# Target rows of an attention stage kept on chip and picked by TensorE's registers, in place of rows loaded for each tile of edges

## The chip, the cores and the metric

The kernel runs on one core of one Trainium2 chip. The metric is the device time of one execution in microseconds (us); the time before is the median of three runs. A core has TensorE (PE, matrix products out of on-chip memory into the accumulation banks called `psum`), VectorE (DVE), ScalarE (ACT), GpSimd (POOL) and SyncE (SP), which issues DMAs. Each engine works through its own list of instructions in order and waits on semaphores for the others.

## The reference, cut to what matters

A graph of 3125 nodes and 50000 edges, the edges sorted by target, goes through two attention layers. The change is in the second one:

```python
x = rms_norm(x) @ W_down                       # 1024 -> 256 features
xl = (x @ Wl).reshape(n, 4, 64)                # row of a node as source
xr = (x @ Wr).reshape(n, 4, 64)                # row of a node as target
msg = xl[src] + xr[dst]                        # one row for each edge
act = where(msg > 0, msg, 0.2 * msg)
e = einsum('ehd,hd->eh', act, att)             # logits, 4 heads
alpha = softmax of e over the edges (and self loop) of one target
out = segment_sum(alpha[..., None] * xl[src], dst)
x = layernorm(x + out.reshape(n, 256) @ W_up)
```

## The kernel before, in words

The edges stand in 440 tiles of 128, four tiles make a group (`U = 4`, 110 groups), five groups a block (`BG = 5`, 22 blocks). A tile of edges has its targets within one window of 64 nodes (`WN = 64`); `wtab` holds the window number of each tile, which depends on the data. From a tile to the next it stays or goes up by one.

**Node stage** (lines 1332 to 1652). For 25 tiles of 128 nodes it finishes layer 0 and makes the rows `xl` and `xr` (256 features and 8 partial logits, `XRW = 264` words). `xl` goes to the table `xl_table` in DRAM. `xr` is written to the on-chip array `acc` (`xr[:, t, :]`) and stored from there to `xr_table` by SP (`store_xr`, L1426 to 1429). At the start of the stage SP also has the table of local target numbers copied from DRAM to DRAM in another order (L1430 to 1432).

**Fused stage** (L1672 to 2176), all engines in one loop over the groups:

- POOL gathers the `xl` rows of a group's edges, four indirect DMAs a group, into a ring of 15 groups (`RG = 15`, helper line L161). It may gather group g once group g - 15 has been weighed.
- SP loads, for every tile of edges, the 64 `xr` rows of its window into `near` (L1770, 66 KB, its address from a register), and for every block the local target numbers `lt` of 640 edges for each half of the partitions (L1762, two DMAs) and the segment masks (L1776, four DMAs).
- ACT makes the transposed one-hot matrices `onehot_t` of group g + 2 from `lt` (L1817, L1819). The two first tiles of a group stand on partitions 0 to 63, the other two on 64 to 127, so they are 128x256 for a group.
- PE (`logits`, L1874 to 1890) forms `xr[dst] + xl[src]` in `psum` by halves of a group: for two tiles `onehot_t` (64 rows) times `near` (L1884), then the identity times the ring (L1889, 128 rows).
- DVE multiplies each half by the attention vector (`product`, L2026), reduces (L2032), and adds to the logits in `finish` (L2039); ACT copies the linear part of the logits (`self_logits`, L1826) after each product and so frees the banks.
- Once for a block a segmented scan over edges gives the softmax weights `pw` (PE L1909 to 1933, DVE L2050 to 2093, ACT L1854 to 1866).
- Ten groups behind (`BACK = 10`) the rows are weighed: per group sixteen pieces of 64 columns (4 tiles, 4 heads); ACT does twelve (L1842), DVE four in one instruction (L2135). PE sums them by target with `onehot` (L1949, 16 matmuls of two 64-column halves) and DVE adds the result to `acc1` (L2112, four times a group). DVE picks the window there by a register that moves on by one bit a tile (`go_on`, L1983 to 1986); the bits are made once by `pack_moves` in block 1 (L1972 to 1981).

**Last stage**: `W_up` and the layer norm, L2227 on.

What sets the order is the text of each engine's loop (`unit`), unrolled by three blocks, and the semaphores: `s_ot` one-hot made, `s_xr` near rows landed, `s_r` gather landed, `s_pg` half a group in `psum`, `s_pd` product read, `s_sc` linear part read, `s_wa` and `s_wd` weighed by ACT and DVE.

Of the kernel before, what the change touches and what calls it, by code (L numbers as in the profile page):

```python
# [308 lines left out]
def gnn_kernel(nc, x, src, dst, w0, att_s, att_d, bias, rms_w, w_down, wl, wr, att1, w_up, out):  # L309
# [9 lines left out]
    xr_t = nc.dram_tensor("xr_table", (NP, XRW), F32, kind="Internal").ap()  # L319
    wloc2_t = nc.dram_tensor("window_local_blocks", (T // 20, 2, 10 * P), BF16, kind="Internal").ap()  # L320
# [18 lines left out]
    with top:  # L339
# [989 lines left out]
        accf = acc[:].rearrange("p t n -> p (t n)")  # L1329
        xr = accf[:, 0:NT * XRW].rearrange("p (t n) -> p t n", n=XRW)  # L1330
        att_relu = w9[:].rearrange("p t n -> p (t n)")[:, 3 * D + HID:3 * D + 2 * HID]
        with ExitStack() as ph:
# [39 lines left out]
            s_xrs = sem("n_xrs")  # L1372
            s_wl2 = sem("n_local_blocks")
# [8 lines left out]
            with nc.Block() as block:  # L1382
# [18 lines left out]
                def _(sp):  # L1401
# [31 lines left out]
                    pipelined(sp, NT, [(0, load_sums), (0, load), (0, load_down), (8, store_xr)],  # L1433
                              AHEAD, 6)
                    sp.wait_ge(s_wl2, 32)
                    sp.wait_ge(s_xrs, 16 * NT)
# [121 lines left out]
                def _(dve):  # L1558
                    sums = Chain(dve, s_zc)
                    nc.vector.tensor_scalar(isrc[:], isrc[:], int(MISS) - 1, None, ALU.bitwise_and)  # L1560
                    dve.wait_ge(S["zt"], 1)
# [93 lines left out]
        BG = 5  # L1655
        BS = BG * U
        NBLK = NG // BG
# [5 lines left out]
        acc1 = accf[:, NWP * P:NWP * P + NWP * 2 * HS].rearrange("p (w h n) -> p w h n", w=NWP, h=2)  # L1663
        FREE = NWP * (P + 2 * HS)
# [4 lines left out]
        assert FREE2 <= NT * D - 2 * D  # L1669
        s_last = [sem("f_" + n) for n in ("wu", "xl")]  # L1670
        s_x1 = [sem(f"f_x1{i}") for i in range(2)]
        with ExitStack() as ph:  # L1672
# [14 lines left out]
            in_xl = Words(accf, 0, NWP * P)  # L1687
# [3 lines left out]
            near = in_xl.take(BG * 2 * XRW).rearrange("p (s q n) -> p s q n", s=BG, q=2)  # L1691
# [52 lines left out]
            with nc.Block() as block:  # L1744
# [11 lines left out]
                def _(sp):  # L1756
# [22 lines left out]
                    def unit(u, r, k, m):  # L1779
# [5 lines left out]
                        for i in range(BG):  # L1785
# [7 lines left out]
                            if k < NBLK - 1 and i == 1:  # L1793
                                load_local(u + 1, (r + 1) % RU)
                            if i == 2:
                                load_masks(u, r)
# [582 lines left out]
```

## Time and profile before

| | us |
|---|---|
| median of three runs | 2523.01 |
| lowest, highest | 2516.96, 2532.45 |
| the profiled execution's own time | 2534.76 |
| its span, first to last instruction | 2533.1 |

| engine | busy us | share of the span |
|---|---|---|
| PE | 1896.9 | 75% |
| DVE | 1597.8 | 63% |
| ACT | 1183.2 | 47% |
| POOL | 1063.6 | 42% |

The profile comes from one execution, which took 2534.76 us; 1.66 us of it lie outside the span. Its mean granted TensorE clock is 0.891 of full speed. By the line numbers in the timeline the stages are: preparation and logits of layer 0 up to about 526 us, the first aggregation up to 1247, the node stage to 1464, the fused stage to 2425, the last stage to the end. The shares of busy time are means over these stages, so a stage has to be read by its own rows.

### The profile page before, as it was taken

The numbers are of one execution on the slowest core, as the hardware profiler recorded it, in microseconds if no ns is written. First come the engines' busy times: TensorE is split into PE (matmuls) and PEld (weight loads), VectorE is DVE, ScalarE is ACT, GpSimd is POOL, SyncE is SP. The second block draws the span as 40 slices with busy tenths as digits, with TensorE's granted clock in tenths as the row PEclk, the third lists the DMA queues.
The fourth block names the chain that finished last, engine by engine and source line by source line (L and its number), as shares of the span: only waits on it lengthen the run. The fifth ranks groups of instructions, "written<-read, shape, count | busy, mean of one in ns | idle before, by whom it ended". The sixth has DMA issues, their size and how long they took to land. (4 is left out here: it accounts for less than half of the span.)

```text
span 2533.1 us, 50983 instructions
## 1 busy us (share of the span) xinstructions
PE 1896.9 (75%) x12291; PEld 1206.5 (48%) x12291; DVE 1597.8 (63%) x4381; ACT 1183.2 (47%) x4251; POOL 1063.6 (42%) x1564
## 2 busy tenths in 40 slices
PE   5899999866777766677588924776777677777778
PEld 4455555334555444445377712444444444444443
DVE  6677777555555555555589815666666665666768
ACT  3100000246665665666566601554555554555766
POOL 1122222146666666666311162455454555454140
PEclk9999999979999999999889966888777887888779
DMA  8444433068888888888799743444344443444547
GB/s 316 107 101 111 109 103 97 33 211 286 289 287 285 292 287 290 288 286 289 232 314 330 233 127 87 109 111 110 105 112 106 115 115 106 109 109 104 97 146 264
DMA packets 209857, 456.49 MB, mean 180 GB/s; under 512 B 41915, under 2 KB 111288, under 8 KB 209648
## 3 DMA queue, kind: packets, MB, share of 16 engines
q0 software_dynamic: 90000, 281.90, 34.8%
q1 hardware_dynamic: 89008, 144.64, 19.1%
q10 hardware_dynamic: 30672, 27.93, 5.1%
q8 instruction: 70, 1.15, 0.2%
q14 instruction: 107, 0.88, 0.1%
HBM read 419.97 MB, written 47.44 MB: 185 GB/s over the span
## 5 line engine op out<-in xcount | busy, mean ns | idle before, releaser
L161 POOL DMA_INDIRECT ring<-xl_table,isrc x440 | 447.2, 1016 | 449.8 <-DVE w L2135 198.4
L1270 ACT ACTIVATE wone<-onehot,w 128x64 f32<-128x64 f32 x1760 | 433.8, 334 | 288.5 <-DVE onehot L1316 166.9
L1287 PE MATMUL banks<-w_sb,wone 128*64 128x256 f32 x2368 | 342.8, 415 | 142.9 <-DVE acc L1312 55.1
L161 POOL DMA_INDIRECT w_sb<-xp_table,isrc x296 | 297.6, 1005 | 180.0 <-PE banks L1290 107.1
L995 PE MATMUL banks<-w_sb,acc 128*128 128x512 f32 x736 | 342.1, 604 | 0.0
L1842 ACT ACTIVATE w<-ring,pw 128x64 f32<-128x64 f32 x1320 | 325.5, 335 | 0.0
L1884 PE MATMUL banks<-acc 64*128 64x264 f32 x880 | 194.4, 523 | 156.8 <-ACT lg L1826 50.8
L1312 DVE TENSOR_TENSOR acc<-banks,acc 128x512 f32 x440 | 304.5, 692 | 0.0
L1889 PE MATMUL banks<-ring,ident 128*128 128x260 f32 x880 | 301.4, 472 | 2.2 <-issue 2.2
L2026 DVE SCALAR_TENSOR_TENSOR acc<-banks,w 128x512 f32<-128x512 f32 x220 | 146.2, 686 | 238.4 <-remote 134.8
L1311 DVE TENSOR_TENSOR zacc<-banks,zacc 64x9 f32 x440 | 69.5, 158 | 330.6 <-PE banks L1290 210.5
L1287 PEld LDWEIGHTS banks<-w_sb,wone 128*64 128x64 f32 x2368 | 179.1, 145 | 198.9 <-issue 80.8
L1949 PE MATMUL banks<-w,acc 128*64 128x132 f32 x1760 | 157.9, 333 | 123.0 <-DVE w L2135 111.0
L1826 ACT ACTIVATE lg<-banks 128x16 f32<-128x16 f32 x220 | 42.7, 198 | 442.2 <-DVE acc L2026 345.0
L1889 PEld LDWEIGHTS banks<-ring,ident 128*128 128x128 f32 x880 | 175.8, 222 | 121.4 <-issue 101.5
L1287 PE MATMUL banks<-rows_c,wone 128*64 128x256 f32 x1152 | 159.9, 403 | 71.5 <-DVE acc L1312 24.7
L2112 DVE TENSOR_TENSOR acc<-banks,acc 128x132 f32 x440 | 127.3, 289 | 108.7 <-remote 72.0
L1884 PEld LDWEIGHTS banks<-acc 64*128 64x128 f32 x880 | 82.3, 224 | 232.4 <-issue 203.2
L1949 PEld LDWEIGHTS banks<-w,acc 128*64 128x64 f32 x1760 | 126.0, 166 | 138.9 <-DVE acc L2119 114.7
L995 PEld LDWEIGHTS banks<-w_sb,acc 128*128 128x128 f32 x736 | 131.2, 191 | 122.1 <-issue 122.0
L161 POOL DMA_INDIRECT rows_c<-xp_table,isrc x144 | 144.5, 1004 | 86.8 <-PE banks L1290 49.6
L931 ACT ACTIVATE zacc<-pidx 128x450 f32<-128x450 f32 x1 | 0.6, 578 | 361.9 <-DVE onehot_t L1081 361.9
(343 smaller groups left out, 2938.7 us busy)
## 6 DMA issues: line engine op xcount, KB each, us to landing
acc<-xr_table SPq DMA_DIRECT2D x440, 66.0 KB
lt_bc<-local_dst ACTq DMA_DIRECT2D x110, 128.0 KB, 3.7
w<-acc SPq DMA_DIRECT2D x100, 128.0 KB, 4.5
x_table<-y POOLq DMA_DIRECT2D x25, 512.0 KB, 7.2
acc<-x_table SPq DMA_DIRECT2D x25, 512.0 KB, 3.7
low_bc<-src_low ACTq DMA_DIRECT2D x98, 128.0 KB, 4.3
acc<-in_x SPq DMA_DIRECT2D x12, 1024.0 KB, 13.2
xp_table<-xp_st SPq DMA_DIRECT2D x24, 512.0 KB
```

The costliest lines, as they stand in the source:

```text
L161: return self.pool.indirect_dma_start(out, None, table, bass.IndirectOffsetOnAxis(ap=idx, axis=0), bounds_check=self.bound, oob_is_err=False)
L995: last = nc.tensor.matmul(psum[:, 2 * r + i], xT_all[:, u, k, :], w_sb[:, k, i * 512:(i + 1) * 512], start=(k == 0), stop=(k == KD - 1))
L1270: last = nc.scalar.activation(wone[:, s, j, h, :], onehot[:, s, j, :], ACT.Copy, scale=w9[:, bass.ds(g * U + j, 1), h:h + 1].rearrange("p ...
L1287: nc.tensor.matmul(psum[WN * a:WN * (a + 1), j, k * C:(k + 1) * C], wone[:, s, j, h, :], slots[r][:, j, h * C:(h + 1) * C], start=True, st ...
L1311: nc.vector.tensor_tensor(zv, psum[0:WN, 4 + j, 0:W9], zv, ALU.add)
L1312: nc.vector.tensor_tensor(av, psum[:, j, :], av, ALU.add).then_inc(s_acc, 1)
L1842: last = nc.scalar.activation(msg[:, s, j, h, 0:HD], ring[:, rg * U + j, h * HD:(h + 1) * HD], ACT.Copy, scale=pw[:, r2, i2 * U + j, h:h + 1])
L1884: nc.tensor.matmul(psum[:, 2 * e + j // 2, 0:XRW], onehot_t[half, rg % 3, j % 2, :], near[half, i, j % 2, :], start=True, stop=False)
L1889: last = nc.tensor.matmul(psum[:, 2 * e + j // 2, 0:XLW], ident[:], ring[:, rg * U + j, :], start=False, stop=True)
L1949: last = nc.tensor.matmul(sums_of(j)[WN * a:WN * (a + 1)], onehot[:, s, j, :], msg[:, s, j, 2 * a:2 * a + 2, :].rearrange("p h n -> p (h n)"),
L2026: nc.vector.scalar_tensor_tensor(out=prod[:, 2 * e:2 * e + 2], in0=psum[:, 2 * e:2 * e + 2, 0:HID], scalar=0.0, in1=bc(att_relu[:].unsquee ...
L2112: nc.vector.tensor_tensor(v, sums_of(j), v, ALU.add).then_inc(s_acc, 1)
```

## The change

`xr` isn't stored any more: it stays in `acc`, and the second layer's logits read it there. `onehot_t` gets one column block for each tile of edges and all 128 partitions (128x512 for a group), and its product with `xr` is a matmul of 128 rows against the tile of 128 nodes that holds the window. PE picks that tile with registers: `place` counts windows, `place >> 1` is the tile, and one bit per tile of edges moves it on. `pack_moves` is made in the node stage, so that PE and DVE both read the packed words. `lt` is one broadcast of 2560 numbers to 128 partitions for a block (640 KB) from a table that exists already. Halves of a group are now tiles 0, 1 and 2, 3. ACT weighs ten of a group's sixteen pieces, DVE six, in two instructions.

```diff
-    xr_t = nc.dram_tensor("xr_table", (NP, XRW), F32, kind="Internal").ap()
-    wloc2_t = nc.dram_tensor("window_local_blocks", (T // 20, 2, 10 * P), BF16, kind="Internal").ap()
...
-                    def store_xr(t, s, m):
-                        sp.wait_ge(S["sf"], t + 1)
-                        sp.dma_start(xr_t[bass.ds(t * P, P), :], xr[:, bass.ds(t, 1), :].rearrange("p a n -> p (a n)"))\
-                          .then_inc(s_xrs, 16)
-                    for a in range(2):
-                        sp.dma_start(wloc2_t[:, a].rearrange("b (i n) -> b i n", n=2 * P),
-                                     wloc_t.rearrange("(b i a q) e -> a b i (q e)", i=5, a=2, q=2)[a]).then_inc(s_wl2, 16)
...
-                    sp.wait_ge(s_wl2, 32)
-                    sp.wait_ge(s_xrs, 16 * NT)
...
                     nc.vector.tensor_scalar(isrc[:], isrc[:], int(MISS) - 1, None, ALU.bitwise_and)
+                    link = Chain(dve, s_pack)
...
+                    for s in reversed(range(BS - 1)):
+                        link(nc.vector.scalar_tensor_tensor(out=packed, in0=packed, scalar=2.0, in1=by_block[:, :, s],
+                                                            op0=ALU.mult, op1=ALU.add))
+                    link(nc.vector.tensor_copy(packed_i, packed))
                     dve.wait_ge(S["zt"], 1)
...
-        acc1 = accf[:, NWP * P:NWP * P + NWP * 2 * HS].rearrange("p (w h n) -> p w h n", w=NWP, h=2)
-        FREE = NWP * (P + 2 * HS)
+        acc1 = accf[:, NT * XRW:NT * XRW + NWP * 2 * HS].rearrange("p (w h n) -> p w h n", w=NWP, h=2)
+        FREE = NT * XRW + NWP * 2 * HS
...
-            onehot_t = in_wu.take(3 * 2 * P).rearrange("p (s q e) -> p s q e", s=3, q=2)
+            onehot_t = between.take(3 * U * P).rearrange("p (s j e) -> p s j e", s=3, j=U)
...
-            ACT_MORE = U
+            ACT_MORE = 2
...
                     def load_local(b, r):
                         wait(sp, s_ot, (b - RU + 1) * BG)
-                        for a in range(2):
-                            sp.dma_start(lt[WN * a:WN * (a + 1), r].rearrange("p i n -> p (i n)"),
-                                         wloc2_t[bass.ds(b, 1), a].rearrange("b n -> (b n)").partition_broadcast(WN))\
-                              .then_inc(s_lt[r], 16)
-
-                    def load_near(g, i, at):
-                        wait(sp, s_pg, 2 * (g - BG + 1))
-                        for j in range(U):
-                            half = slice(WN * (j // 2), WN * (j // 2 + 1))
-                            sp.dma_start(near[half, i, j % 2, :], xr_w[bass.ds(at[j], 1)].rearrange("w n c -> (w n) c"))\
-                              .then_inc(s_xr[i], 16)
+                        sp.dma_start(lt[:, r].rearrange("p i n -> p (i n)"),
+                                     local_t[b * BS:(b + 1) * BS, :].rearrange("s e -> (s e)").partition_broadcast(P))\
+                          .then_inc(s_lt[r], 16)
...
+                    pe.reg_mov(place, 0)
+                    pe.reg_load(words, packed_i)
+
+                    def tile_of_step(word):
+                        pe.reg_alu(moved, place, 1, ALU.logical_shift_right)
+                        tile = pe.snap(moved, min_val=0, max_val=NT - 1)
+                        pe.reg_alu(moved, word, 1, ALU.bitwise_and)
+                        pe.reg_alu(place, place, moved, ALU.add)
+                        pe.reg_alu(word, word, 1, ALU.logical_shift_right)
+                        return tile
+
                     def logits(g, r, i, m):
                         rg = BG * r + i
+                        at = [tile_of_step(words[g // BG]) for j in range(U)]
                         pe.wait_ge(s_ot, g + 1)
-                        pe.wait_ge(s_xr[i], 64 * (RU * m) + 64 * r + 64)
                         for e in range(2):
                             wait(pe, s_pd, 2 * (g - 1) + e + 1)
                             wait(pe, s_sc, 2 * (g - 1) + e + 1)
-                            for j in (e, e + 2):
-                                half = slice(WN * (j // 2), WN * (j // 2 + 1))
-                                nc.tensor.matmul(psum[:, 2 * e + j // 2, 0:XRW], onehot_t[half, rg % 3, j % 2, :],
-                                                 near[half, i, j % 2, :], start=True, stop=False)
+                            for j in (2 * e, 2 * e + 1):
+                                nc.tensor.matmul(psum[:, j, 0:XRW], onehot_t[:, rg % 3, j, :],
+                                                 xr[:, bass.ds(at[j], 1), :].rearrange("p a n -> p (a n)"),
+                                                 start=True, stop=False)
```

**PE, one group of the fused stage, before.** The names in brackets are semaphores (their numbers are used again through the program, so a name can be that of an earlier use); `acc` is where `near` and `onehot_t` lie.

```order
L1884 MATMUL banks<-acc 128x264 [waits p1_lg,p1_es,scan_m,p1_pg]
L1884 MATMUL banks<-acc 128x264
L1889 MATMUL banks<-ring,ident 128x260 [waits p2_r2_0]
L1889 MATMUL banks<-ring,ident 128x260
L1884 MATMUL banks<-acc 128x264 [waits p1_es,p1_lg]
L1884 MATMUL banks<-acc 128x264
L1889 MATMUL banks<-ring,ident 128x260 x2
L1909 MATMUL banks<-ident,lg 80x128 [waits b_wv,b_m,p1_onehot_hi]
```

The same place now (L1881 is L1889 of before, L1902 is L1909):

```order
L1860 ISA
L1862 REGISTER_ALU
L1863 ISA
L1862 REGISTER_ALU
L1863 ISA
L1875 ISA [waits p1_lt3,p1_lt4,p1_lt1]
L1875 MATMUL banks<-acc 128x264
L1875 ISA
L1875 MATMUL banks<-acc 128x264
L1881 MATMUL banks<-ring,ident 128x260 [waits rows_cleared]
L1881 MATMUL banks<-ring,ident 128x260
L1875 ISA [waits p1_lt3,p1_lt4]
```

The pair L1862, L1863 stands four times in the program, twice is shown. So the matmuls are as many as before and in the same places, one semaphore less is waited for at the first, and thirteen rows of register work come with each group: nine ahead of the first matmul, and one ahead of each of the four that read `xr`.

**SP, one group and what a block adds, before:**

```order
L1762 DMA acc<-window_local_blocks 64x1280 [waits p1_pg]
L1762 DMA acc<-window_local_blocks 64x1280
L1770 ISA [waits p1_at]
L1770 DMA acc<-xr_table 64x264
L1770 ISA
L1770 DMA acc<-xr_table 64x264
L1770 ISA
L1770 DMA acc<-xr_table 64x264
L1770 ISA
L1770 DMA acc<-xr_table 64x264
L1776 DMA acc<-segment_ends 20x256 x4
```

A whole block of five groups now:

```order
L1751 DMA acc<-local_dst 128x2560 [waits p1_lt1]
L1758 DMA acc<-segment_ends 20x256 [waits s_w0]
L1758 DMA acc<-segment_ends 20x256 x3
```

In a block of before twenty pairs of a register row and an L1770 stand beside the L1762 and L1776; of these 46 rows five are left.

## Rows read from the trace of the kernel before

**Rows 1.** Windows: busy us of each engine (count), PEclk, DMA share, GB/s, by stage.

```profile
540.00:1240.00 700.00, 497.85 (x4304) 348.14 (x4302) 378.74 (x967) 421.96 (x1712) 432.59 (x431) 0.95 0.86 288
1240.00:1464.00 224.00, 174.42 (x912) 144.32 (x907) 183.29 (x542) 133.38 (x294) 27.25 (x52) 0.92 0.85 270
1465.00:1597.00 132.00, 53.40 (x226) 30.44 (x228) 47.55 (x108) 22.14 (x74) 62.44 (x62) 0.67 0.40 105
1597.00:2383.00 786.00, 576.67 (x3438) 361.27 (x3438) 504.19 (x1425) 437.47 (x1755) 384.73 (x379) 0.82 0.41 107
```

**Rows 2.** Groups by line and form, 1597 to 2383: busy us, mean ns, idle before.

```profile
L2032 DVE TENSOR_REDUCE part<-acc 128x16 f32<-128x1024 f32 x100 | 121.3, 1213 | 0.6 <-issue 0.6
L2112 DVE TENSOR_TENSOR acc<-banks,acc 128x132 f32 x396 | 114.4, 289 | 92.2 <-remote 72.0 <-PE banks L1949 4.1 <-issue 3.5
L1819 ACT ACTIVATE acc<-acc,edge 128x256 f32<-128x256 f32 x98 | 49.8, 508 | 6.2 <-remote 3.1
L1842 ACT ACTIVATE w<-ring,pw 128x64 f32<-128x64 f32 x1183 | 291.8, 335 | 0.0
```

**Rows 3.** Waits, 1597 to 2383: who waited for whom, us in total, times, longest.

```profile
DVE acc L2026 <- remote: 111.6, 36, 6.7
DVE acc L2112 <- remote: 72.0, 27, 7.2
DVE acc L2026 <- PE banks L1889: 43.6, 33, 4.3
...
PE banks L1949 <- DVE w L2135: 95.0, 43, 4.5
...
POOL ring L161 <- DVE w L2135: 198.4, 40, 8.5
```

**Rows 4.** Timeline, 1907 to 1917.5: start, us, instruction, [idle before <-releaser].

```profile
1907.31 1.01 POOL L161 DMA_INDIRECT ring<-xl_table,isrc  x1 [3.60 <-issue]
...
1911.47 1.15 PE L1889 MATMUL banks<-ring,ident 128*128 128x260 f32 x4
...
1916.13 0.69 DVE L2026 SCALAR_TENSOR_TENSOR acc<-banks,w 128x512 f32<-128x512 f32 x1 [4.29 <-PE banks L1889]
```

**Rows 5.** Timeline of the fused stage's start, DVE, SP's queue and POOL.

```profile
1476.12 0.69 DVE L2026 SCALAR_TENSOR_TENSOR acc<-banks,w 128x512 f32<-128x512 f32 x1 [10.72 <-issue]
...
1502.88 51.11 SPq L1770 DMA_DIRECT2D acc<-xr_table  x16
...
1518.61 0.69 DVE L2026 SCALAR_TENSOR_TENSOR acc<-banks,w 128x512 f32<-128x512 f32 x1 [22.00 <-issue]
...
1542.84 1.01 POOL L161 DMA_INDIRECT ring<-xl_table,isrc  x1 [0.30 <-issue]
```

**Rows 6.** Timeline, PE in the fused stage at 2362 and in the node stage.

```profile
2361.96 0.72 PE L1884 MATMUL banks<-acc 64*128 64x264 f32 x4
2362.61 1.15 PE L1889 MATMUL banks<-ring,ident 128*128 128x260 f32 x4
2363.68 0.26 PE L1916 MATMUL banks<-tails,w 80*4 80x20 f32 x4
...
1382.50 0.60 PE L1550 MATMUL banks<-wlr,hT 128*128 128x260 f32 x2
1382.94 0.60 PE L1552 MATMUL banks<-wlr,hT 128*128 128x260 f32 x2
```

**Rows 7.** One line's instructions, L971 (layer 0, PE's sequencer): ns, minimum, median, maximum.

```profile
L971 PEldq FUSED_REGOPS  x440: 46/46/46, 96.3 to 466.2; - x147
```

**Rows 8.** Waits of DVE, first aggregation, and its timeline at 544.

```profile
DVE zacc L1311 <- PE banks L1290: 198.5, 113, 3.2
...
544.24 0.16 DVE L1311 TENSOR_TENSOR zacc<-banks,zacc 64x9 f32 x1 [6.67 <-PE banks L1290]
```

**Rows 9.** Timeline of the packing in block 1, and of the node stage's start.

```profile
1565.53 4.27 DVE L1979 SCALAR_TENSOR_TENSOR acc<-acc 1x22 f32<-1x22 f32 x19
...
1256.99 1.70 ACT L1461 ACTIVATE w<-w,rz 128x256 f32<-128x256 f32 x4 [4.12 <-DMA w<-acc]
```

More of the change, by code:

```diff
@@ L1652, in _ @@
                               AHEAD, 6)
-        BG = 5
-        BS = BG * U
-        NBLK = NG // BG
         BR = BS * H
@@ L1715, in gnn_kernel @@
             edge = sb("edge6", [P, 2])
-            packed_i = sb("packed6", [P, NBLK], I32)[32:33, :]
-            moves, packed = between.take(T)[32:33], between.take(NBLK)[32:33]
-            upper = sb("upper6", [P, 1])
             s_lt = [sem(f"q_lt{i}") for i in range(3)]
-            s_xr = [sem(f"q_xr{i}") for i in range(BG)]
             s_mk = [sem(f"q_mask{i}") for i in range(3)]
             s_r = [sem(f"q_r{i}") for i in range(RG)]
-            (s_first, s_edge, s_const, s_zero, s_ab, s_ot, s_pg, s_sc, s_pd, s_pt, s_lg, s_au0, s_au, s_aut, s_any, s_pack) = (
-                sem("q_" + n) for n in "first edge const zero ab ot pg sc pd pt lg au0 au aut any pack".split())
+            (s_first, s_edge, s_const, s_zero, s_ab, s_ot, s_pg, s_sc, s_pd, s_pt, s_lg, s_au0, s_au, s_aut, s_any) = (
+                sem("q_" + n) for n in "first edge const zero ab ot pg sc pd pt lg au0 au aut any".split())
             (s_t1, s_sl, s_ck, s_fb, s_t2, s_c, s_fd, s_fe, s_t3, s_m, s_f, s_ff, s_e, s_t4, s_wv, s_ws) = (
@@ L1783, in unit @@
                             return
-                        at = windows.load(u)
-                        for i in range(BG):
-                            load_near(BG * u + i, i, at[i * U:(i + 1) * U])
-                            if k == 0 and i == 0:
-                                sp.dma_start(ends[0:TB], mask_t.rearrange("(b p) k e -> p b k e", b=NB)).then_inc(s_first, 16)
-                                with nc.allow_non_contiguous_dma(reason="the first edge of each block"):
-                                    for h in range(H):
-                                        sp.dma_start(first16[h:h + 1, :],
-                                                     wloc_t.rearrange("(b s) e -> e b s", s=BS)[0:1, :, 0]).then_inc(s_first, 16)
[L1793 to L1796, printed above, removed]
+                        if k == 0:
+                            sp.dma_start(ends[0:TB], mask_t.rearrange("(b p) k e -> p b k e", b=NB)).then_inc(s_first, 16)
+                            with nc.allow_non_contiguous_dma(reason="the first edge of each block"):
+                                for h in range(H):
+                                    sp.dma_start(first16[h:h + 1, :],
+                                                 wloc_t.rearrange("(b s) e -> e b s", s=BS)[0:1, :, 0]).then_inc(s_first, 16)
+                        load_masks(u, r)
+                        if k < NBLK - 1:
+                            load_local(u + 1, (r + 1) % RU)
                     units(unit)
@@ L1873, in _ @@
                     pe.wait_ge(s_const, 2)
+                    words = [pe.alloc_register(f"q1_word{b}") for b in range(NBLK)]
+                    place = pe.alloc_register("q1_place")
+                    moved = pe.alloc_register("q1_moved")
+                    pe.reg_mov(place, 0)
[7 more added lines that the diff above has]
+                        return tile
                     def logits(g, r, i, m):
                         rg = BG * r + i
+                        at = [tile_of_step(words[g // BG]) for j in range(U)]
                         pe.wait_ge(s_ot, g + 1)
-                        pe.wait_ge(s_xr[i], 64 * (RU * m) + 64 * r + 64)
                         for e in range(2):
```

53 lines of the change are left out of this document (23 added, 30 removed).

## The prediction, made before the changed kernel was run

> **What bounds the kernel now.** I read the windows by stage first, since the change touches the fused stage and, a little, the node stage. In the steady part of the fused stage no engine is full [rows 1]: in 786 us PE is busy 576.67, DVE 504.19, ACT 437.47 and POOL 384.73. The reduce ran 100 times there [rows 2], so a group takes 7.9 us, and of that PE works 5.8, DVE 5.0, ACT 4.4 and POOL, with 1.01 us a gather and 0.30 between two [rows 4, 5], 5.2 for four. The order of the engines' work and the waits between them set the 7.9, so I read the waits next.
>
> The largest wait of an engine that is needed all the time is DVE's, 111.6 us before its product L2026 and 72.0 before its add L2112, both put down to "remote", which says that no engine's last instruction explains them [rows 3]. The timeline shows what they are like: PE's second half of a group ends at 1911.47 + 1.15 = 1912.62, but DVE's product on it starts at 1916.13 [rows 4]. POOL stands in an unbroken run of gathers at that time. I call these 184 us the holds. Everything downstream is paced by them: PE waits 95.0 us for DVE's weighing and POOL 198.4 us for the same instruction [rows 3].
>
> The start of the fused stage shows the same, drawn out. The ring is empty, so POOL issues 60 gathers in a row, at 1.31 us 78.6 us of them, the last at 1542.84; SP needs 51.11 us for sixteen near loads in that time; DVE stands idle 22.00 us before the product at 1518.61 [rows 5]. In the first aggregation SP issues no such loads, POOL works more of the time (432.59 of 700 us against 384.73 of 786 [rows 1]), and DVE's longest wait for PE there is 3.2 us [rows 8]. Yet the first run of gathers of that stage has a wait of 6.67 us too [rows 8]. So the holds belong to POOL's runs, and whether SP's loads have a part in them is what the trace leaves open. It is the largest open term.
>
> **The change part by part.** The sum is made against the profiled execution, 2534.76 us, which lies 11.8 above the median of 2523.01; the differences are then taken from the median.
>
> *Packing.* Nineteen steps in a chain take 4.27 us in block 1 [rows 9], with their two neighbours some 5. Products of DVE stand behind them there. In the node stage they come when ACT waits 4.12 us for a DMA [rows 9] and DVE for ACT. **-5** (-5 to 0).
>
> *Node stage.* 25 stores and two DMAs go. DVE is busy 183.29 of 224 us and the DMA engines 85% [rows 1]; the stores run beside DVE's work. **0** (-3 to +2).
>
> *Start of the fused stage.* The products at 1476.12 and 1518.61 are the first and the fourth [rows 5]: 14.2 us for a half group, so five in the 67 us that POOL's run still lasts. If PE no longer waits for near rows and a half takes the 6.67 us of the one hold seen with SP quiet [rows 8], ten pass: 2.5 groups more, at 7.9 us some 20 us. Against it, the first one-hots wait for a broadcast of 640 KB where 160 KB were; at 107 GB/s [rows 1] that is 6 us. **-13** (-30 to +6).
>
> *DVE's weighing.* An instruction of 128x128 is added to each group. The nearest row is the 128x132 add at 289 ns [rows 2]: 0 if all of it falls into DVE's idle time, 31 us over 110 groups if none does. PE or POOL waited for that weighing 43 and 40 times in 100 groups [rows 3], so I put most of it on the path: **+25**.
>
> *ACT.* Two pieces fewer are 2 x 291.8/1183 = 0.49 us saved a group [rows 2]. The two one-hot instructions double in columns: from 508 ns [rows 2] each comes to between that and twice that, so 0 to +1.0 us a group. ACT works 4.4 of 7.9 us; net **0**, hidden by its idle time. If that cover went, the worse end would be 0.5 x 110 = +55 us.
>
> *PE, the matmuls.* Now four records of the 64-row product take 2361.96 to 2362.61 = 0.65 us and four of the identity 1.07 [rows 6], 1.72 a half group. In the node stage two records of 128x260 come every 0.44 us [rows 6], so eight take 1.76. That is +0.04 a half, +9 us over 220 halves. Low end 0; high end, if the identity's product stays at 1.07, 0.23 x 220 = 51. I take **+10**, because the node stage's row is of the same shape and of one kind following another, as after the change.
> The Trainium skill, "TensorEngine Tiling (Array Packing)", Theoretical Speedup, says that products with a contraction of 64 or less gain up to 2x by being set side by side, which speaks against this change; by it the sum would be 134 us worse than by the row (rival 4). Its Key Properties add that changing the tiling mode drains TensorE; the 1.07 against 0.88 for four 260-column records agrees.
>
> *PE, the registers.* Thirteen rows a group. The nearest row is a register operation of PE's sequencer at 46 ns [rows 7]: 0.60 us a group, 66 us if nothing hides it. Nine of them stand behind the sixteen sums matmuls of the group before, one before each xr product, where 46 ns is less than the 220 of a record. PE has 2.1 us idle in each group too. **0** (0 to 66).
>
> *DMA.* Near loads of 66 KB, 20 a block, and 320 KB of local numbers give way to 640 KB. The DMA engines are 41% busy [rows 1]: **0** by itself.
>
> *The holds.* 184 us in the steady part. If SP's 40 rows a block are their cause, nearly all go, and the wait that comes next, DVE's for PE, 43.6 us now [rows 3], grows: I bound the gain by 150. If POOL's run alone is the cause, nothing goes, since the gathers and what frees them are unchanged. The aggregation stage speaks for the first, its beginning for the second; I take a third: **-60** (-150 to 0).
>
> Sum: -5 - 13 + 25 + 10 - 60 = -43, so 2534.76 would be 2492, and the median **2480**.
>
> **The rivals.**
> 1. *All holds go* (the fast case). For: no "remote" wait in the aggregation, with POOL busier. Against: the 6.67 us at its start. -43 - 90 gives **2390**; a group then takes about 6.7 us.
> 2. *The holds stay whole*; near loads were hidden. For: POOL's 60 gathers and each run stay. -43 + 60 = +17: **2540**.
> 3. *TensorE's path decides, slower.* The place is between the last sums matmul of one group and the first xr product of the next. If the sequencer can't run the nine register rows while the array works, each group waits. PE is waited for by DVE, DVE's product frees ACT and the banks, so its time lies on the loop even with PE not full. Price: holds whole +17, and 66: **2606**. It decides once the gap there grows by more than 0.07 us, the 8 us over 110 groups that rival 2 leaves to the 1% line. For: PE is the busiest engine, and here registers feed the address of the very next matmul. Against: 46 ns, and 2.1 us of idle time.
> 4. *The 64-row products lose all of their side by side.* The 0.65 us become 1.30 at each half: 143 in place of 9, from 2480 to **2614**. Against: 128-row records at 0.22. This is the skill's rule as told above.
> 5. *The change doesn't do what it says*: the near loads were replaced in time by lt's broadcasts and the fused stage waits for these. 640 KB at 107 GB/s are 6 us of a block's 39: no change, **2525**.
>
> **How the numbers follow.** A measurement of this kernel tells about 1%, 25 us, from no change: three runs lie within 15. Chances: forecast 0.32 (2450 to 2510), all holds go 0.17, holds stay 0.22, TensorE's path 0.19, side by side lost 0.06, no effect 0.04. Faster than 2498: 0.29 of the forecast, 0.17 of rival 1, 0.01 elsewhere: 0.47. Slower than 2548: rivals 3 and 4, 0.25, and 0.06 of rival 2, with the ACT cover gone or the weighing dearer: 0.31. Within: 0.22. The likeliest case's own range is 2450 to 2510. The range for 8 in 10 leaves out some 0.08 below (rival 1 with the start of the stage at its best) and 0.11 above: **2390 to 2610**.
>
> **What would show it.** Right: "remote" before L2007 and the add at about 120 us instead of 184; a group at 7.5 us; the nine register rows of PE not in front of an idle array; eight records of a half in 1.76 us; ACT at 4.4 us a group; DVE 0.25 more. The start, from 1465 to the tenth reduce, 13 us shorter. Wrong: "remote" unchanged (rival 2) or gone (rival 1); PE's idle time before L1875 put down to "issue" and 0.6 us a group (rival 3); half groups at 2.4 us (rival 4). What would upset all of it is a wait that only the new order makes: PE's registers need words packed much earlier, and ACT's longer one-hots stand ahead of the copy that frees the banks.

## The result, and the profile after

The changed kernel took 2520.75 us (median of 20 runs, 2512.68 to 2530.07) and the kernel before, timed 20 times, 2534.39 (2516.96 to 2546.70). The ratio is 0.9948, 95% interval 0.9929 to 0.9967: 13 us faster, less than the 1% that the prediction calls no change. The prediction had 43 us. The profiled execution took 2518.04 us, its span is 2516.4, at a clock of 0.910, against 2534.76 and 2533.1 before.

By stage (windows, columns as in [rows 1]; the fused stage now starts at 1466 and its steady part ends 19 us earlier):

```profile
1240.00:1465.00 225.00, 178.61 (x958) 148.92 (x955) 190.07 (x570) 136.98 (x309) 27.16 (x52) 0.92 0.80 256
1466.00:1585.00 119.00, 56.66 (x222) 43.10 (x223) 42.18 (x81) 26.21 (x70) 62.13 (x62) 0.69 0.34 99
1585.00:2364.00 779.00, 578.88 (x3442) 445.57 (x3440) 524.09 (x1527) 432.07 (x1556) 383.51 (x379) 0.90 0.29 81
```

The node stage is as long as it was, with the packing (DVE 190.07 for 183.29 us) inside. From the first gather to the tenth reduce there are 113.0 us for 125.2, so 12 of the 17 us by which the spans differ come from the start; the other hundred groups gain 7: DVE works 20 us more there, and 7.85 us go to a group in place of 7.99 (from the fifteenth reduce to the 109th). The waits and groups of the steady part:

```profile
DVE acc L2007 <- DMA lt_bc<-local_dst: 108.3, 34, 5.0
DVE acc L2007 <- PE banks L1881: 70.8, 38, 4.3
DVE acc L2093 <- remote: 30.9, 16, 5.5
...
PE banks L1875 <- ACT lg L1804: 84.1, 62, 3.6
PE banks L1942 <- DVE w L2116: 67.9, 40, 4.0
...
POOL ring L161 <- DVE w L2116: 243.8, 52, 8.4
...
L1797 ACT ACTIVATE acc<-acc,edge 128x512 f32<-128x512 f32 x98 | 70.7, 722 | 3.2
L2116 DVE TENSOR_TENSOR w<-ring,pw 128x128 f32<-128x128 f32 x99 | 29.1, 293 | 1.4 <-issue 1.4
```

The 34 waits of the first line are put down to a DMA of layer 0 that had long landed, so they are what "remote" was in [rows 3]: no instruction explains them. By these labels unexplained are 108.3 + 30.9 = 139 us, for 184 before. But the waits for PE grew from 43.6 to 70.8, and with the 10.1 of "issue" in L2007 DVE's idle time before the product and the add is 189.5 + 51.4 = 241 us against 160.2 + 92.2 = 252.

The labels mislead here, and already did in [rows 4]: the product at 1916.13 is put down to PE, whose last record had ended at 1912.62. So I count without them what I call the held time. A product or an add could start when DVE's last instruction and PE's last matmul record for the same banks have both ended (the ends of PE's records are modelled). Where it starts over 1 us later, the difference is held time, summed from the tenth to the 109th reduce. Before it is 137 us at the products and 69 at the adds, 206 in all; now 168 and 30, 198 in all. The holds have hardly shrunk. Of the 70.8 us of waits for PE some 58 pass after PE was done, of the 43.6 before some 33. Two instructions have the price that was expected: the one-hot of 128x512 takes 722 ns, the added weighing 293.

What such a hold looks like now (timeline: start, us, instruction):

```profile
2153.70 1.05 PE L1875 MATMUL banks<-acc 128*128 x4
2154.59 1.04 PE L1881 MATMUL banks<-ring,ident 128*128 128x260 f32 x4
...
2156.66 0.69 DVE L2007 SCALAR_TENSOR_TENSOR acc<-banks,w 128x512 f32<-128x512 f32 x1 [1.28 <-PE banks L1881]
...
2160.11 1.01 POOL L161 DMA_INDIRECT ring<-xl_table,isrc  x1 [0.30 <-issue]
2162.37 0.69 DVE L2007 SCALAR_TENSOR_TENSOR acc<-banks,w 128x512 f32<-128x512 f32 x1 [5.01 <-DMA lt_bc<-local_dst]
```

PE has the group's second half ready at 2155.63, the product of the first ends at 2157.35, and the one of the second starts at 2162.37, 1.25 us after POOL's eighth gather in a row has ended (2161.12). I count pauses under 0.75 us as inside a run. Of 45 waits of over 2.4 us before a product or an add in the steady part 26 end 0.5 to 1.5 us after the end of a run of gathers, stretches that make up less than a tenth of the time, and 18 more end inside a run, mostly of eight. In the kernel before it is 19 and 20 of 47. So the run is the thing to test, and PE is the second: its register rows stand in front of a waiting array, as the spacing in experiment 4 shows.

### The profile page after: what moved, and what is told of

The parts are those of the page before. It is cut to its first block and busy times, and to the rows that moved or that the text cites. A ratio compares the mean times of both kernels' runs of the same rounds, so it can differ in the third digit from the quotient of the medians.

```text
span 2516.4 us, 50722 instructions
## 1 busy us (share of the span) xinstructions
PE 1911.3 (76%) x12291; PEld 1310.3 (52%) x12291; DVE 1620.2 (64%) x4490; ACT 1177.4 (47%) x4031; POOL 1061.0 (42%) x1564
## 5 line engine op out<-in xcount | busy, mean ns | idle before, releaser
L1285 PE MATMUL banks<-w_sb,wone 128*64 128x256 f32 x2368 | 350.6, 421 | 148.0 <-DVE acc L1310 55.9
L1875 PE MATMUL banks<-acc 128*128 x880 | 283.4, 451 | 190.2 <-ACT lg L1804 88.9
L2007 DVE SCALAR_TENSOR_TENSOR acc<-banks,w 128x512 f32<-128x512 f32 x220 | 146.2, 687 | 261.8 <-DMA lt_bc<-local_dst 146.8
L1875 PEld LDWEIGHTS banks<-acc 128*128 128x128 f32 x880 | 177.0, 215 | 256.8 <-issue 230.5
L1820 ACT ACTIVATE w<-ring,pw 128x64 f32<-128x64 f32 x1100 | 273.1, 334 | 0.0
L1881 PE MATMUL banks<-ring,ident 128*128 128x260 f32 x880 | 258.0, 420 | 2.4 <-DMA ring<-xl_table,isrc 2.4
L1804 ACT ACTIVATE lg<-banks 128x16 f32<-128x16 f32 x220 | 43.2, 197 | 430.7 <-DVE acc L2007 333.2
L1942 PE MATMUL banks<-w,acc 128*64 128x132 f32 x1760 | 144.7, 314 | 93.8 <-DVE w L2116 85.2
L1881 PEld LDWEIGHTS banks<-ring,ident 128*128 128x128 f32 x880 | 188.0, 214 | 40.8 <-DMA ring<-xl_table,isrc 3.2
L1942 PEld LDWEIGHTS banks<-w,acc 128*64 128x64 f32 x1760 | 115.3, 155 | 107.3 <-issue 104.6
L2093 DVE TENSOR_TENSOR acc<-banks,acc 128x132 f32 x440 | 127.6, 290 | 67.7 <-remote 30.9
L1288 PEld LDWEIGHTS banks<-w,onehot 128*64 128x64 f32 x880 | 127.7, 146 | 81.5 <-issue 26.7
```

What stands on the lines that cost most here:

```text
L1285: nc.tensor.matmul(psum[WN * a:WN * (a + 1), j, k * C:(k + 1) * C], wone[:, s, j, h, :], slots[r][:, j, h * C:(h + 1) * C], start=True, st ...
L1288: nc.tensor.matmul(psum[0:WN, 4 + j, 0:W9], onehot[:, s, j, :], w9[:, bass.ds(i, 1), :].rearrange("p a n -> p (a n)"), start=True, stop=Tr ...
L1820: last = nc.scalar.activation(msg[:, s, j, h, 0:HD], ring[:, rg * U + j, h * HD:(h + 1) * HD], ACT.Copy, scale=pw[:, r2, i2 * U + j, h:h + 1])
L1875: nc.tensor.matmul(psum[:, j, 0:XRW], onehot_t[:, rg % 3, j, :], xr[:, bass.ds(at[j], 1), :].rearrange("p a n -> p (a n)"), start=True, st ...
L1881: last = nc.tensor.matmul(psum[:, j, 0:XLW], ident[:], ring[:, rg * U + j, :], start=False, stop=True)
L1942: last = nc.tensor.matmul(sums_of(j)[WN * a:WN * (a + 1)], onehot[:, s, j, :], msg[:, s, j, 2 * a:2 * a + 2, :].rearrange("p h n -> p (h n)"),
```

## The experiments

Ratios are to the kernel before on the same chip, with 95% intervals. The kernels ran on five occasions, on two kinds of chip. On three of them, as in the first result, the kernel before takes 2489 to 2554 us. On the two others its median is 2093 and 2094. I call the first "with holds": on the second no unexplained wait of DVE is seen. Each experiment says where it ran.

### 1. Shorter runs by a wait

```diff
                         for j in range(U):
+                            if j == 2:
+                                gather.wait(s_pt, g - BG + 1)
                             gather.rows_of(ring[:, g % RG * U + j, :], xl_t, ...
```

> The changed kernel, but POOL waits before the third gather of group g until DVE has reduced group g - 5, so that its runs are two to four gathers in place of eight. In the changed kernel's trace the held product starts 11.6 us after a run of eight begins, some 1.3 us after its end, again and again. Theory 1 (runs): what holds DVE is an unbroken run of gathers; broken runs take most of the 139 us of unexplained waits before L2007 and the add away, and the start of the fused stage, where 60 gathers stand in a row, gets 20 to 40 us shorter: ratio to the kernel before 0.95 to 0.975. Theory 2 (loads and engines' own work): runs only coincide with the waits, and the pacing delays gathers for nothing: ratio 0.99 to 1.01.

It ran without holds: 1.0135 (1.0119 to 1.0150). There is nothing to take away there, so it told of the chip only. Once more:

> The paced kernel of the first call once more. On a chip near 2093 us it was slower (1.0135). On a chip near 2530 us, theory 1 (the holds belong to unbroken runs of gathers) expects 0.95 to 0.975, with the unexplained waits before L2007 and the add mostly gone; theory 2 (the runs only coincide) expects 1.0 to 1.02.

With holds: 0.9891 (0.9859 to 0.9924), 0.65% below the changed kernel on the same chip, and short of the 0.95 to 0.975 that theory 1 expected. The start of the stage, with its 60 gathers in a row, is 95.0 us long to the tenth reduce for 114.9: runs of 26, 12, 12, 12 and 8 stand there now. The steady part is not faster (7.91 us a group), and the edit hardly did there what was meant: from 1600 to 2340 22 of its 62 runs are still eight long and 20 six, where the changed kernel on that chip has 28 of 65 eight long. The held time is 193 us for 192. So theory 1 is borne out at the start, where the run was broken, and not tested in the steady part.

### 2. No near loads in the kernel before

```diff
                             if k == 0:
                                 load_near(BG * u + i, i, at[i * U:(i + 1) * U])
...
-                        pe.wait_ge(s_xr[i], 64 * (RU * m) + 64 * r + 64)
+                        pe.wait_ge(s_xr[i], 64)
```

> The kernel before, but SP loads near rows in the first block alone and the later blocks read those again (this leaves the loads of 420 of 440 windows out, so the logits are of wrong rows); all else is as before. Theory 2 (SP's loads have a part in the holds): the unexplained waits of DVE fall by a third or more and the time by 30 to 100 us, ratio 0.96 to 0.99. Theory 1 (POOL's runs alone): the waits stay near 184 us in the steady part, the ratio is 0.995 to 1.0, and what gain there is lies at the start of the stage.

Without holds: 0.9999 (0.9989 to 1.0010), a group takes 5.43 us.

> The kernel before without near loads after the first block once more (those loads are left out, so logits are of wrong rows). On the chip without holds it changed nothing (0.9999). On a chip near 2530 us, the prediction's step (SP's loads have a part in the holds, a third of 184 us) expects a ratio of 0.96 to 0.98 and unexplained waits before L2026 and L2112 near 120 us; if the loads have no part, the waits stay near 184 us and the ratio is 0.993 to 1.0, the start of the stage being all that gains. On a chip near 2093 us: 1.0 again.

With holds: 0.9873 (0.9814 to 0.9933), some 32 us, between the two expectations. Waits of DVE there, 1600 to 2300:

```profile
DVE acc L2027 <- remote: 78.2, 24, 5.0
DVE acc L2027 <- PE banks L1890: 55.6, 29, 3.6
DVE acc L2113 <- remote: 44.8, 24, 4.4
```

123 us in 700, where [rows 3] has 184 in 786, 164 for 700: a quarter less. The held time is 173 us for 206. The start of the stage gained nothing: to the tenth reduce it takes 125.9 us, and the products come as they did before, 22 us apart:

```profile
1487.22 0.69 DVE L2027 SCALAR_TENSOR_TENSOR acc<-banks,w 128x512 f32<-128x512 f32 x1 [11.65 <-remote]
1492.08 30.55 SPq L1770 DMA_DIRECT2D acc<-xr_table  x8
1509.15 0.69 DVE L2027 SCALAR_TENSOR_TENSOR acc<-banks,w 128x512 f32<-128x512 f32 x1 [21.24 <-remote]
```

This doesn't clear the near loads at the start, though: the edit keeps the first block's twenty, and the last eight of them run right through that wait. What does show that such a wait needs no near load is the changed kernel, which has none. SP issues nothing there from 1475 to 1547, and DVE still waits 21.64 us:

```profile
1544.95 0.69 DVE L2007 SCALAR_TENSOR_TENSOR acc<-banks,w 128x512 f32<-128x512 f32 x1 [21.64 <-DMA lt_bc<-local_dst]
```

### 3. The division of the weighing

```diff
-            ACT_MORE = 2
+            ACT_MORE = U
```

> The changed kernel, but ScalarE weighs twelve of sixteen pieces as before, VectorE four in one instruction. By the prediction's term, 0.23 us of DVE a group lie on the path: 25 us faster than the changed kernel, ratio to the kernel before about 0.985. If DVE's work is hidden by its waits, or ACT's longer one-hots need the relief, no change or slower: ratio 0.995 to 1.0.

Without holds: 1.0076 (1.0062 to 1.0090), a group takes 5.71 us. The changed kernel itself wasn't run on such a chip, so this gives no difference by itself.

> The kernel before, with ten pieces of sixteen weighed by ScalarE and six by VectorE, the change's division alone. The prediction put 25 us on it (ratio 1.01). If DVE's idle time covers it: 1.000 to 1.003. If ACT was the one that was waited for (on a chip without holds, ACT is busy some 80% in this stage): below 1.

The reverse edit on the kernel before, with holds: 0.9999 (0.9972 to 1.0026). The ten-piece division costs nothing there. DVE's idle time before products and adds, from the tenth to the 109th reduce, is 157 + 77 us where the kernel before on that chip has 155 + 94, so the 293 ns fall at least in part into DVE's waits.

### 4. No register work on PE

```diff
-                        at = [tile_of_step(words[g // BG]) for j in range(U)]
...
-                                                 xr[:, bass.ds(at[j], 1), :].rearrange("p a n -> p (a n)"),
+                                                 xr[:, g * NT // NG:g * NT // NG + 1, :].rearrange("p a n -> p (a n)"),
```

> The changed kernel, but PE reads a tile of target rows that is fixed in the program, with no register work in the fused stage (this leaves out the choice by data, so some logits are of wrong rows). If the thirteen register rows a group are hidden, as predicted, the ratio stays 0.995 (0.99 to 1.0). If they lie on PE's path at 46 ns each, 66 us go: ratio 0.97.

Without holds: 1.0047 (1.0033 to 1.0060), a group takes 5.61 us.

> The changed kernel with a fixed tile of target rows and no register work on PE once more (logits of wrong rows). On the chip without holds the ratio was 1.0047. On a chip near 2530 us: 0.995 if the registers are hidden there, as predicted, 0.97 if all 66 us of them are on the path.

With holds: 0.9819 (0.9760 to 0.9879). To have both on one chip:

> The changed kernel again, to stand on one chip beside the one with a fixed tile. On a chip with holds 0.995; on one without them 1.008 to 1.012.

> The changed kernel with a fixed tile, no register work on PE (logits of wrong rows), on one chip with the changed kernel. If the registers are on PE's path in part, it is 0.8 to 1.3% below the changed kernel (20 to 33 us of the 66 bounded); if the difference of the earlier runs came from the chips, the two agree within 0.3%.

The changed kernel took 2495.45 us, 0.9960 (0.9937 to 0.9982), the one with a fixed tile 2453.74, 0.9799 (0.9774 to 0.9825): **42 us** (some 33 to 50), and it is more than the "in part" of the expectation. One load of the packed words ahead of the stage is all that is left of the registers. The timelines show it. PE in the changed kernel:

```profile
1802.45 1.12 PE L1942 MATMUL banks<-w,acc 128*64 128x132 f32 x16
1803.98 1.15 PE L1875 MATMUL banks<-acc 128*128 x4 [0.41 <-issue]
1804.97 1.04 PE L1881 MATMUL banks<-ring,ident 128*128 128x260 f32 x4
1805.84 1.05 PE L1875 MATMUL banks<-acc 128*128 x4
1806.73 1.04 PE L1881 MATMUL banks<-ring,ident 128*128 128x260 f32 x4
1807.61 0.38 PE L1902 MATMUL banks<-ident,lg 128*80 128x128 f32 x2
```

and with the fixed tile:

```profile
1810.16 1.12 PE L1941 MATMUL banks<-w,acc 128*64 128x132 f32 x16
1811.21 1.16 PE L1874 MATMUL banks<-acc 128*128 128x264 f32 x4
```

From the first of the sixteen sums records to the first xr record it is 1.05 us without the registers, as in the kernel before (1912.76 to 1913.81), and 1.53 with them. From the last sums record the median of some 90 groups is 0.21 and 0.75 us, 0.54 apart; in the kernel before it is 0.36, waits included. Ten of the thirteen rows stand ahead of the first xr product, 0.46 us at 46 ns, and the 0.41 of "issue" above is nine of them, so the rows were hardly hidden at all; what makes up the rest of the 0.54 isn't shown. The sixteen matmuls of 132 columns go out every 70 ns; that they leave little under which register rows could run is my reading.

The held time falls too, from 183 us to 113 (132 in the fixed kernel's trace on the earlier occasion). How the 42 us divide between the longer spacing and the longer holds that come with it isn't shown.

### 5. The changed kernel and the kernel before again

> The changed kernel itself, to have it, the kernel before and the experiments side by side on one chip. The chip of the first four experiments ran the kernel before in 2093 us where the first profile has 2535, with no unexplained waits of DVE at all. If this chip is like the first profile's (kernel before at 2520 to 2550): ratio 0.995, and the unexplained waits are there. If it is like the second (2093): there is no hold to take away, and by what the twelve-piece kernel (1.0076) and the fixed tile (1.0047) showed, the ratio is 1.008 to 1.012.

With holds: 0.9956 (0.9932 to 0.9979). The forecast for this repeat, and the first result, hold.

> The kernel before, for a trace of it on this chip. On a chip with a time near 2093 us its group should take 5.4 us in the fused stage as the kernel without near loads did (5.43), against 7.99 in the first profile; on a chip near 2530 us it should repeat the first profile.

2538.02 us, 7.91 us a group, 125.4 us to the tenth reduce; unexplained waits of 117.8 and 74.2 us from 1600 to 2385: the first profile's picture.

### 6. A pause on POOL

```diff
                         for j in range(U):
+                            if j in (0,):
+                                nc.gpsimd.memset(rest[:], 0.0).then_inc(s_rest, 1)
+                                rests[0] += 1
+                                pool.wait_ge(s_rest, rests[0])
                             gather.rows_of(...
```

The scratch tile `rest` is 128x1024.

> The changed kernel, but POOL clears a scratch tile of 128x1024 before each group's four gathers and waits for it, so that no run of gathers is longer than four, with about 1.3 us between two. Nothing is left out. If the length of a run is what holds DVE, the waits that end 11.6 us after a run's start can't come about any more: on a chip near 2530 us the ratio falls to 0.93 to 0.97. If the holds come with any gather, whatever the length, the pause is a loss: 1.0 to 1.02. On a chip near 2093 us, where POOL is the engine without idle time, the pause costs up to 1.3 us a group, ratio 1.03 to 1.08.

With holds: **0.9194** (0.9139 to 0.9249), 2304.19 us for 2504.37. Better than expected. A group takes 6.30 us, the tenth reduce comes after 68.2 us for 115. Windows and waits (1620 to 2140) and POOL's groups (1600 to 2100):

```profile
1620.00:2140.00 520.00, 429.08 (x2865) 339.94 (x2866) 434.38 (x1270) 363.30 (x1307) 421.57 (x416) 0.98 0.38 105
```

```profile
DVE acc L2100 <- remote: 34.7, 26, 2.7
```

```profile
L161 POOL DMA_INDIRECT ring<-xl_table,isrc x320 | 329.1, 1028 | 94.8 <-issue 73.2 <-POOL rest L1748 19.2 <-DVE w L2123 2.4
L1748 POOL MEMSET rest<- 128x1024 f32 x80 | 77.6, 970 | 0.0
```

No run is longer than four, the waits labelled "remote" fall to 34.7 us in 520 and none is over 2.7, the held time falls to 45 us, PE's clock rises from 0.90 to 0.98, and POOL now waits for the weighing 2.4 us in 500: it is the engine that sets 6.3 us. The same edit on the kernel before:

> The kernel before with POOL's pause of 1.3 us before each group's gathers, all else as it was. With the changed kernel the same pause gave 0.919 on a chip with holds. If the holds belong to POOL's runs alone, 0.915 to 0.925 here too. If near loads add to the holds, the kernel before gains less: 0.93 to 0.95. If the change had costs that the holds hid, it gains more: 0.90 to 0.915, unless POOL, full at 6.3 us a group in the paused kernel, sets the pace of both.

With holds: 0.9452 (0.9417 to 0.9488), a group 6.82 us. It gains less, as "near loads add to the holds" said. Its waits, 1620 to 2140:

```profile
DVE acc L2119 <- remote: 33.8, 14, 4.5
DVE acc L2033 <- remote: 32.3, 22, 2.6
```

66 us where the changed kernel has 35; by held time 96 for 45. So runs of four still hold DVE, for shorter. With the pause the changed kernel is ahead by 0.9194/0.9452 = 0.973 (0.966 to 0.980, the two intervals put together, from two occasions). So what the change gives is worth more once the runs are short. A shorter pause (128x256):

> The changed kernel with a pause a quarter as long (a clear of 128x256, about 0.3 us) before each group's gathers. POOL then is full at about 5.6 us a group instead of 6.3. If any break in the run lets DVE's waits end, a group takes 5.8 to 6.0 us and the ratio is 0.90 to 0.905. If the length of the pause matters, holds come back: above 0.93.

With holds: 0.9834 (0.9798 to 0.9870). Any break isn't enough:

```profile
L1748 POOL MEMSET rest<- 128x256 f32 x65 | 20.6, 318 | 127.2 <-DVE w L2123 119.1 <-issue 8.1
```

Where POOL doesn't wait for the weighing, there are now 0.6 us between two groups' gathers, against 0.3 within a group, and long-held products again start 6.5 or 10 us after such a run of eight has begun. The held time is 141 us. A pause of 1.3 us was enough and one of 0.6 wasn't; between them nothing was tried with holds.

### 7. Plain transfers in place of gathers

```diff
-                            gather.rows_of(ring[:, g % RG * U + j, :], xl_t, isrc[...]).then_inc(s_r[g % RG], 16)
+                            t = (g * U + j) % (NT - 1)
+                            pool.dma_start(ring[:, g % RG * U + j, :], xl_t[t * P:(t + 1) * P, :]).then_inc(s_r[g % RG], 16)
```

> The changed kernel, but each gather of 128 rows by index is a plain DMA of 128 rows in a row from POOL's queue (this leaves the gathering in the fused stage out; the sources' rows are wrong). If the gathers, which POOL itself works on for 1.0 us each, cause the unexplained waits, these go altogether and a group takes 5.0 to 5.6 us on any chip: 240 to 300 us less on a chip near 2530. If transfers as such cause them, they stay, with the period near 7.9 us.

With holds: 0.8994 (0.8940 to 0.9048), a group 5.83 us, above the expected 5.6. Its largest waits of DVE, 1620 to 2140, and POOL:

```profile
DVE acc L2007 <- PE banks L1881: 21.6, 33, 0.8
DVE acc L2093 <- PE banks L1942: 11.8, 10, 1.6
```

```profile
L1745 POOL DMA_DIRECT2D ring<-xl_table x308 | 163.4, 537 | 283.7 <-DVE w L2116 276.5 <-issue 7.1
```

As many bytes go to the ring, no wait is unexplained there, and the held time is 0. At the stage's start 60 such transfers are issued in a row in 31.74 us, and the tenth reduce comes after 58.4 us for 115. The holds come with the gathers by index, not with the transfers as such. What it is in a gather isn't shown: POOL also works half as long on a plain transfer (537 ns for 1028), and the rows it reads lie side by side.

### 8. Registers loaded from a table

```diff
-                    pe.reg_load(words, packed_i)
+                    tiles = StepTiles(pe, dtab, "q1", BS)
+                    loaded = []
...
-                        at = [tile_of_step(words[g // BG]) for j in range(U)]
+                        if g % BG == 0:
+                            loaded[:] = tiles.load(g // BG)
+                        at = loaded[g % BG * U:(g % BG + 1) * U]
```

> The changed kernel, with PE's registers loaded once a block from the table of tile numbers that layer 0 left on chip (one load of 20 words), in place of nine rows of register arithmetic a group; nothing is left out. If those rows are what the fixed tile saved, the spacing from the last sums matmul to the first xr matmul falls from 0.75 to about 0.3 us and the ratio, on a chip with holds, is 0.98 to 0.986. If the loads, 22 of them, cost 1 to 2 us each where they stand, 0.985 to 0.993. If varying the tile was the cost, 0.996.

Without holds: 1.0141 (1.0120 to 1.0162). The spacing is 0.21 us as meant, but each load of twenty words makes PE wait:

```profile
L1866 PE MATMUL banks<-acc 128*128 x663 | 183.1, 399 | 16.7 <-issue 16.7
```

16.7 us in 16 blocks of that window, 1.04 each, so 0.21 a group, and its group takes 5.83 us where the fixed tile took 5.61. So the spacing is that of the nine arithmetic rows, and the two kernels differ by about what the loads cost, which leaves little for the choice of tiles by data. They ran on two chips of that kind, and on a chip with holds this kernel wasn't run.

> The same with POOL's pause, three quarters as long as in the first paused kernel (a clear of 128x768). With the long pause POOL was full at 6.3 us a group and the ratio was 0.919. POOL would now be full at 6.0 us: 0.90 to 0.91 if the break still suffices. If it doesn't, holds come back as in the kernel with the short pause (0.983) and the ratio is above 0.94.

Without holds: 1.0246 (1.0225 to 1.0267), 6.02 us a group, POOL's own 6.0. What the two give together on a chip with holds stays open.

## Why the prediction was right or wrong

**Right: the range, the sign and the reading of what binds.** No engine was full, and the holds paced the stage. They go with POOL's runs, and leaving the near loads out takes a part of them and not the whole.

**The step that failed: "PE, the registers: 0".** Measured 42 us (2495.45 to 2453.74), two thirds of the 66 that I had as the upper end. Both reasons given fell. Nine rows behind sixteen sums matmuls are not hidden: the spacing there is 0.54 us a group longer than without them. PE's 2.1 us of idle time a group didn't take them up either. It is rival 3's place and mechanism with a smaller price. This one term takes the forecast of -43 to -1. It is also what the forecast missed by: with the fixed tile the kernel is 52 us below the kernel before (2453.74 for 2505.72; by the ratio 50, 44 to 57), so all the rest of the change together gives some -50, where the rest of the sum has -43. That is also why rival 3's sign didn't come: it had +17 for that rest.

That the rest came near as a sum is in part luck: its terms miss in both directions, as follows.

**Mis-sized, and badly founded: "the holds: -60".** Leaving the near loads out gave -32 (interval -47 to -17) together with all else that they do. The labels' 184 to 139 us looks like -45, but the held time went only from 206 to 198. The evidence for a third was read wrongly. I took it that the first aggregation, where SP issues no near loads, has no such waits, and counted that against POOL's runs. It has them (545 to 1240, kernel before):

```profile
DVE zacc L1311 <- DMA w_sb<-in_L_gnn_W: 67.6, 30, 4.2
```

That DMA brought weights in the first 25 us of the program, so these are 67.6 us of unexplained waits under another name than "remote". On a chip without holds (first run of experiment 2, 500 to 1100) the line is missing. POOL's runs in the aggregation are mostly five or six gathers with some 1.9 us between; the pause shows for the fused stage that shorter runs with such breaks leave shorter holds.

**Mis-sized: "DVE's weighing: +25".** The instruction is 293 ns, as said; on the kernel before it costs 0.9999, thus 0 with 7 us either way. I took the waits for L2135 as a sign that DVE's work is on the path, but its idle time in holds takes it up.

**Too large, cause open: "start: -13".** The start is 12.2 us shorter, but the packing's 5, which the sum has as a term of its own, lie in it, so 7 are left for the 13. DVE's wait of 22 us is there without near loads too, as the changed kernel shows. What the 7 come from wasn't tried. (Two slips in the term: its own figures, 20 less 6, make 14, and local numbers of before were 320 KB and not 160.)

**Matmuls: +10 was low.** In the changed kernel's rows the first half of a group takes 0.99 + 0.87 us and the second 0.89 + 0.88, so 3.63 a group for 3.44 before: +21 us at the pace of these rows, within the bounds (0 to 51). I had taken both halves at the pace of one kind following another. But PE's busy time in the steady part is 578.88 us for 576.67: its granted clock there rose from 0.82 to 0.90, and little of this price is left in the trace. Rival 4, that the 64-row products lose all of their side by side, has no sign in the trace.

**Right: the node stage**, within 1 us, with the packing in it. **ACT** is as busy as said (432.07 us for 437.47), but PE's waits for its copy L1804, behind longer one-hots now, are 84.1 us for 40.5 before; what that costs wasn't tried.

The terms taken singly: -32 near loads, +42 registers, 0 weighing, -5 packing, +21 matmuls by their spacing: +26. The kernel is 13 faster. The 39 us between are more than the intervals make together (15, 8 and 7: some 18). The matmuls' 21, of which PE's busy time shows only 2, and the 7 at the start may be a good part of it; that isn't shown, and the rest is unattributed. The terms depend on one another and on the chip: with the pause the same change is worth 2.7%, and where there are no holds near loads cost nothing (0.9999) and both relatives of the changed kernel are slower than the kernel before (1.0047 without register work, 1.0076 with the old division).

## What to carry to other kernels

Sequencer rows are not free because their engine is idle elsewhere: look at what stands right ahead of them, and if those are short matmuls as here, put full price into the sum until a run says otherwise. A wait that nothing explains should be matched with what the other engines do in that time, run by run, before it is put down to one of them. And don't search for it by one label: here the same waits stood under "remote", under a DMA that had long landed and under PE. A cheap pause is worth trying against a long run of gathers by index, on the chip that is meant: on one kind it took 5.5% off the kernel before and brought the changed one to 8% below it, and on the other a shorter one cost 1.1% (2146.43 us for 2123.58).

## What the runs showed of the hardware

The kernel before takes 2093 us or 2490 to 2550 by the chip, with the same gather time (1.01 us, 0.30 between) on both. By the trace of the kernel without near loads, which cost nothing there, some 140 of the 440 us lie ahead of the fused stage (its first gather comes at 1326 instead of 1465), the most of the rest in its groups: 5.43 us against 7.99. Some 135 of the 140 are in the first aggregation, the other stage with many gathers (its last comes at 1100 instead of 1235): from 540 to 1140 350 GB/s are moved, against 289 in the kernel before with holds. The node stage is about as long on both.

On a chip with them, DVE's product and add often start well after PE has written their banks. In the changed kernel 44 of 45 such waits of over 2.4 us end inside a run of gathers or 0.5 to 1.5 us after its end; they are shorter with runs of four and 1.3 us between (held time 45 us for 183 to 198), and absent with plain transfers. Why one kind of chip has them is open.

TensorE's granted clock went from 0.82 to 0.90 with the change and to 0.98 with the pause in the steady part, that is more time at 2.4 GHz and less at 1.2. PE's idle stretches of over 3 us went from 101 us in 740 (1600 to 2340) to 47 with the change, and there is none with the pause (1600 to 2140).
